# Attention sums of the second key tile of each unit in one piece of 512 queries

## What is computed

```python
q = _apply_rope(q, cos, sin)
k = _apply_rope(k, cos, sin)
inv_scale = 1.0 / jnp.sqrt(jnp.asarray(D, jnp.float32))
scores = jax.nn.softmax(jnp.einsum('bhqd,bhkd->bhqk', q, k) * inv_scale, axis=-1)
out = jnp.einsum('bhqk,bhkd->bhqd', scores, v)
```

## Time and profile before

| | us |
|---|---|
| median of 3 runs | 3414.24 |
| lowest and highest | 3413.72, 3414.84 |
| the profiled execution, its time | 3415.28 |
| the profiled execution, its span from first to last instruction | 3413.7 |
| PE busy in it | 3345.3 |
| DVE busy in it | 2985.4 |
| ACT busy in it | 2490.2 |

### The profile page before, as it was taken

The page is one execution under the profiler, slowest core; times in us unless marked ns, Lnnn a source line. Parts: engine busy times, 40 slices in busy tenths (PEclk is TensorE's granted clock), DMA queues, the critical chain, the costliest instruction groups (busy, mean ns, idle before and its releaser), DMA issues.

```text
span 3413.7 us, 66851 instructions
## 1 busy us (share of the span) xinstructions
PE 3345.3 (98%) x28054; PEld 1528.5 (45%) x28054; DVE 2985.4 (87%) x3116; ACT 2490.2 (73%) x4521; POOL 128.0 (4%) x288
## 2 busy tenths in 40 slices
PE   9689999999999999999999999999999999999998
PEld 5333333333333333333333333333333288888887
DVE  8999999999999999999999999999999145555554
ACT  5248888888888888888888888888888922222222
POOL 0000000000000000000000000000000000000000
PEclk9679999999999999999999999999999999999999
DMA  4200000000000010001001000000002020000000
GB/s 157 76 4 12 13 12 13 25 15 17 25 12 14 11 62 12 13 13 62 13 11 31 14 12 12 14 13 12 13 8 95 9 96 26 26 26 26 26 13 13
DMA packets 47618, 92.04 MB, mean 27 GB/s; under 512 B 9922, under 2 KB 21828, under 8 KB 47140
## 3 DMA queue, kind: packets, MB, share of 16 engines
q1 hardware_dynamic: 40628, 72.07, 6.6%
q0 software_dynamic: 6688, 15.68, 1.6%
HBM read 69.62 MB, written 28.84 MB: 29 GB/s over the span
## 4 chain that ended last, share of the span: by engine, by line
PE 91%; DVE 5%; ACT 2%; issue 1%; DMA 0%; SPq 0%; DVEq 0%; ACTq 0%
PE sums L680 32%; PE scores L782 25%; PE acc L1121 17%; PE wide L658 13%; DVE group_max L895 2%; PE tok L1168 2%; ACT probs L866 1%; PE tok L1094 1%; DVE pair L305 1%; ACT mixed L846 1%; DVE item L316 1%; DVE pair L313 1%; DVE item L312 1%; PE scores L748 0%; DVE k_all L330 0%
## 5 line engine op out<-in xcount | busy, mean ns | idle before, releaser
L895 DVE TENSOR_REDUCE group_max<-wide 128x2 f32<-128x1024 f32 x2048 | 2473.3, 1223 | 18.2 <-PE wide L658 11.6
L866 ACT ACTIVATE probs<-scores 128x512 f32<-128x512 f32 x4046 | 2199.8, 597 | 294.5 <-PE scores L782 43.6
L680 PE MATMUL sums<-probs,v_all 128*17 128x256 f32 (+1 forms) x16120 | 1279.3, 389 | 7.2 <-ACT mixed L846 6.3
L782 PE MATMUL scores<-q_sb,k_all 51*128 51x512 f32 x3968 | 988.7, 495 | 6.7 <-ACT probs L866 5.7
L658 PE MATMUL wide<-k_all,q_sb 48*128 48x512 f32 x4096 | 851.2, 412 | 30.1 <-DVE group_max L895 25.5
L782 PEld LDWEIGHTS scores<-q_sb,k_all 51*128 51x128 f32 x3968 | 370.7, 183 | 843.2 <-ACT probs L866 829.9
L680 PEld LDWEIGHTS sums<-probs,v_all 128*17 128x17 f32 x16120 | 267.3, 95 | 748.0 <-issue 368.3
L658 PEld LDWEIGHTS wide<-k_all,q_sb 48*128 48x128 f32 x4096 | 397.6, 190 | 68.9 <-DVE group_max L895 62.8
L1234 ACT ACTIVATE whole_hid<-acc,scale 128x512 f32<-128x512 f32 x128 | 84.6, 688 | 286.3 <-PE acc L1121 286.1
L1121 PE MATMUL acc<-hid_b,h2T 128*128 128x512 f32 x1024 | 234.9, 390 | 0.0
L1121 PE MATMUL acc<-hid_a,first_h1T 128*128 128x512 f32 x1024 | 233.4, 389 | 0.0
(11 more groups left out here) (121 smaller groups left out, 1075.1 us busy)
## 6 DMA issues: line engine op xcount, KB each, us to landing
q_sb<-q_parts SPq DMA_DIRECT2D x192, 64.0 KB, 2.5
heads<-mixed SPq DMA_DIRECT2D x128, 34.0 KB
xt<-in_xT SPq DMA_DIRECT2D x8, 512.0 KB, 4.4
q_parts<-k_all SPq DMA_DIRECT2D x8, 512.0 KB, 3.3
q_parts<-parts SPq DMA_DIRECT2D x8, 512.0 KB, 3.3
w_words<-in_h1T POOLq DMA_DIRECT2D x32, 128.0 KB, 2.3
w_words<-in_h2T POOLq DMA_DIRECT2D x32, 128.0 KB, 2.3
heads_sb<-heads SPq DMA_DIRECT2D x16, 256.0 KB
```

What stands on the lines that cost most here:

```text
L680: last = pe.matmul(sums[32 * j:32 * j + HD + 1, cols], v_all[:, kt, g, j], probs[(kt * HG + j) % RING][:, cols], start=(kt == 0 and cols.s ...
L782: pe.matmul(scores[(s + e) % BANKS][:], k_all[rows, g * GP + j, n // HG * P:(n // HG + 1) * P], q_sb[g][rows, j], start=True, stop=True).t ...
L866: act.activation(probs[n % RING][:], bank, ACT.Exp, scale=INV_SCALE)\
L895: dve.reduce_max(group_max[:, n], wide[n % 2][:], AX_X).then_inc(wide_free, 1)
```

## The change

In the second key tile (kt = 1) of each of the 31 units that `unit` writes, the two halves of the sums are not made. Instead all four heads' sums of 512 queries are made once, behind both score pairs and both maximum pairs. All other key tiles keep the order they had.

```diff
                     score_pair(n)
                     if groups:
                         max_group(*groups[0])
-                    sums_of_previous(kt, slice(0, CH // 2))
+                    if kt != 1:
+                        sums_of_previous(kt, slice(0, CH // 2))
                     turn_at(n + PAIR)
                     score_pair(n + PAIR)
                     if groups:
                         max_group(*groups[1])
-                    sums_of_previous(kt, slice(CH // 2, CH))
+                    if kt != 1:
+                        sums_of_previous(kt, slice(CH // 2, CH))
+                    else:
+
+                        sums_of_previous(kt)
```

## The result

| | before | after |
|---|---|---|
| median, us (8 runs each) | 3414.78 | 3425.18 |
| lowest and highest | 3413.72, 3417.23 | 3424.53, 3425.79 |
| profiled execution, its time | 3415.28 | 3424.53 |
| its span | 3413.7 | 3422.9 |

The ratio is 1.0028, with a 95% interval from 1.0019 to 1.0037. The kernel became slower by 10.4 us by the medians and by 9.2 us by the spans of the two profiled executions. Forecast were 3424.9 us and +10.6.

A forecast was written before the change was run, and what follows sets the result against it. PE's own row of work was taken as the bound, 1.22 us per half key tile. 30 units at 0.35 us more, 10.5 us, plus 0.1 in the first gave +10.6 us: median 3424.9 us, range 3419 to 3430.

The forecast's parts named there:

- The bound: Steady attention: PE's own work sets the pace, 1.22 us for half a key tile; lost time is not regained.
- (1): Second key tile: the wait on `sums_free`, moved behind the second maximum pair, costs nothing; the copy is done by 1002.52.
- (2): Second key tile: score pair 6, 7 still waits for exponential 4, 1.43 us after pair 4, 5, where it was 1.50.
- the idle case: Score pair 6, 7 starts 0.05 us after exponential 4's end; the other bound, 0.12, costs 2.1 us more.
- (3) and (4): After pair 6, 7: 0.33 us to maximum pair, 0.33 to sums; one piece takes 0.98, not 1.12, saving 0.14.
- The rival by which the piece saves nothing: Second key tile: the one piece of sums takes the two halves' 1.12 us: +14.8 us, 3429; chance 0.05.
- (5) to (7): Behind the place: no wait at pair 8, 9; DVE idles slightly more, has room; first unit costs 0.1 us.
- The sum: Whole kernel: 0.35 us more in each of 30 units, 10.5 us, with the first unit's 0.1: +10.6 us.
- exponential 4 comes earlier: Second key tile: copy no longer delays exponential 4, the loop alone counts: +0.10 us a unit, +3, 3417; chance 0.07.
- The faster rival: Second key tile: exponential 4 done by 1002.30, PE never idles: 0.42 us less a unit, 12.6 in all, 3402; chance 0.03.
- the falling clock: Each unit: PE's 0.76 us of idleness drops the clock to half level: 87 us and the 10.6, 3512; chance 0.03.

The follow-up runs named there:

- The later copy: The changed kernel with ACT's copy of the sums one exponential later, behind exponential 4: 3408.32 us against 3414.94 for the kernel before, ratio 0.9980.
- the sixth key tile: The same change made in key tile kt = 5 of each unit instead of the second: 3421.65 us against 3414.94 for the kernel before, ratio 1.0019.

## Why the prediction was right

**The bound.** PE's own row of work bounds the steady part, and what it loses in a unit is not won back: right for 27 of the 29 units, whose ordinary slots kept their 1.220 us behind the longer stall. But the ordinary slot is not one fixed number: the prediction took 1.22 us as PE's floor, and in two units it was 1.213.

**(1) The wait on the copy goes.** Right: "ACT mixed" is gone from the waits, and nothing waits at the sums in their new place.

**(2) The score pair waits for exponential 4 instead.** Right in mechanism and size: 1.43 us between the pairs, exponential 4 at 0.75 us after its score pair as before, and the reaction 0.05 us after its end (0.052 to 0.054 in all 30 units), the idle case that I chose over 0.12. The later copy shows the share that the copy has in it, 0.25 us; the sixth key tile shows the rest, the loop of 1.18 us that a slot without sums lays open.

**(3) and (4) The rest of the place.** 0.33, 0.33 and 0.98 us, as taken from the earlier trace rows. The reason given for the 0.98 was right too, a change-over less: two halves in a row take the same. The rival by which the piece saves nothing is out. With it goes what the prediction made of the Trainium skill (TensorE: Matmul & The Clock Gate, the section on the 16 sub-arrays), that weight loads pulled ahead of running matmuls would hide the change-over. In the rows of before some loads are ahead, that of a maximum pair starts at 1041.12 for a matmul at 1041.34, and that of the score pair behind the sums is not (1042.23); the 0.14 us is there all the same.

**(5) to (7)** No further wait came up behind the place, DVE's additional idleness bounded nothing, and the clock stayed at its upper level from 400 to 2600 us. In the first unit the place took 4.47 us for 4.27, 0.20 more where the prediction took 0.1.

**The sum.** The place grew by 0.361 us on the mean of 30 units, 10.8 us; the prediction's rounded rows had 0.35 and 10.5. The spans of the two profiled executions differ by 9.2 us. By the starts of the score pairs this is made up so:

| | us |
|---|---|
| the 29 whole units with a copy: the place | +10.5 |
| the same: two of them in the faster pace | -0.9 |
| the same: all their other slots together | +0.4 |
| what stands ahead of the first unit | +0.7 |
| the first unit | -0.9 |
| from the 31st unit to the end, its own place of 0.36 included | -0.6 |

The first unit got shorter in spite of its longer place because it spent less time at the half clock: full clock came 8.8 us after its start (206.6 to 215.4), in before after 11.3 (205.9 to 217.2). By an estimate those 2.5 us less at half the clock are worth 1.2 us. The last unit had less of it too (mean granted clock 0.91 over 20 us from 2700 to 2720, where before had 0.84 over 22 us from 2690 to 2712). The prediction has no term for either. The medians are 10.4 us apart. The mechanism was right, and the 0.36 us a unit bears it out; that the total came within 0.2 us of the forecast is in part luck, since these other terms are as large as 1 us and change from one execution to the next.

**The rivals.** That exponential 4 comes earlier, with +3 us, did not happen, but it was made to happen by moving the copy: at the place its 2.82 us came out exactly. The faster rival and the falling clock are out by the rows above. What the prediction says of frequent small pauses stands in the Trainium skill, TensorE: Matmul & The Clock Gate, in the section on a second HAM failure mode, not in the one on HAM oscillation; 28 pauses of 0.7 us between 400 and 2600 us did nothing of the kind here, the granted clock stayed at 1.00.

**What I expected wrongly** is in the experiments, not in the forecast. The totals of tile five and of the later copy missed though the prices at the place were right, because the pace of the other slots of a unit changed with them. The two kernels with sums ahead of a maximum pair missed because the change-over was priced wrongly.

## What to carry to other kernels

Before moving work out from between two waiting instructions, add up the loop that it hides: reaction, producer and consumer. Here the loop was 1.18 us under a slot of 1.22, so taking the sums out of one slot laid open 0.5 us of idleness, more than the 0.27 us wait that the move removed. When a wait is moved behind other work, look at what the same late producer holds up next: the copy that delayed the sums also delayed exponential 4. Moving the copy on ACT as well took that part out, 0.25 us of the stall; the 0.5 us of the loop stayed.

Where a kernel repeats a slot two thousand times, compare the starts of ordinary slots too before explaining a difference by the place that was edited; 7 ns a slot were worth more than the edit in one of these kernels.

## What was not expected of the hardware

The same slot of instructions ran at two paces, 1.213 and 1.220 us, and a unit kept its pace for some fifty slots. The pattern over the 29 units was the same in two executions of one kernel (the same 22 both times) and in three kernels it goes by the group of heads, so it is not chance of the single execution. What sets it is open. In the faster pace the maximum matmuls took 387 ns throughout, in the slower mostly 397.

A step between kinds of matmul depends on what came before. The first score or maximum pair behind sums took 0.33 us until the next pair, a second pair in a row 0.24 until a third (1019.04 to 1019.28 with the sums ahead), and the last pair before sums 0.32 to 0.43.
